# Store and load quarters alternate in a hex convolution kernel: 256 KB transfers, a semaphore for each stored quarter

## The chip, the cores and the metric

The kernel runs on one core of a Trainium2 chip. The metric is the device time of one execution in microseconds (us), as the median of several runs. The kernel before takes 740.97 us (three runs, 740.41 to 741.33).

## What is computed

The input x holds 2048 images of 64 channels and 16 x 16 pixels in float32 (134.2 MB). The output has the same shape.

```python
def _gn(v, G=32, eps=1e-5):                  # groups of two channels, over all pixels
    g = v.reshape(B_, G, C_ // G, H_, W_)
    m = jnp.mean(g, axis=(2, 3, 4), keepdims=True)
    s = jnp.var(g, axis=(2, 3, 4), keepdims=True)
    return ((g - m) / jnp.sqrt(s + eps)).reshape(v.shape)
...
xp = jnp.pad(x, ((0, 0), (0, 0), (1, 1), (1, 1)))
xp = xp.at[:, :, DST_R, DST_C].set(xp[:, :, SRC_R, SRC_C])      # 30 border pixels wrap round
up, left, right = (_conv(xp, w * mask, b) for ...)              # 4 x 4 taps, stride 2, 5 taps of each kept
out = zeros; out[0::2, 0::2] = up; out[1::2, 0::2] = left; out[1::2, 1::2] = right
return x + out * OUT_MASK
```

So every image is read once, normalised, convolved with three sparse stride-2 filters, and the results are added to the pixels of x that they belong to. All of x is written out, the unchanged pixels too.

## The kernel before, in words

**Chunks and slots.** The batch is cut into 64 chunks (NCHUNK) of 32 images. A chunk lies in SBUF as 128 partitions (2 images x 64 channels) by 16 "pairs" (G = 16) of 256 pixels: 1 KB of each partition for each pair, 2 MB for a chunk. The tensor xs has 8 such slots (SLOTS); chunk k lives in slot k % 8. The convolution's results are added in place in xs (L401), and the slot is then stored from there. So slot k % 8 can take chunk k + 8 only when chunk k has been stored.

**The engines.** For each chunk DVE takes the statistics (bn_stats, L229, a chunk ahead of the rest), works out scale and shift (L237 to L272) and normalises eight of the 16 pairs into tn (L277). ACT normalises the other eight (L313). POOL copies the wrapped border pixels (L411). PE runs the matmuls (L459). ACT carries the PSUM banks to res (L336), two chunks behind (LAG = 2), and POOL adds res into xs (L401). After the four banks of a chunk the semaphore bank_added stands at 4 * (k + 1).

**The transfers.** All transfers of x and of the output are issued by SP, in one order written out by hand (L182 to L214). First come three weight loads (L196), then chunk 0 in four quarters of 512 KB (L199), each with a semaphore that DVE waits on, then the chunks 1 to 6 in halves of 1 MB (AHEAD = 7). After that SP runs a loop over the chunks. For chunk k it stores half 0, loads half 0 of chunk n = k + 7, stores half 1, and loads half 1 of chunk n. The store waits for bank_added (L207). The load waits until both halves of the chunk that was in the slot, which is chunk k - 1, have been stored (L211): there is one semaphore for a slot, and it has to reach 32 for each turn. DVE waits for the half of a chunk whose statistics it takes (L224, L226). At the end SP waits for every slot's semaphore (L214).

The last chunk's two stores are not held to the same value: half 0 goes when the additions to its pairs are done and half 1 when those to the rest are.

Of the kernel before, what the change touches and what calls it, by code (L numbers as in the profile page):

```python
# [16 lines left out]
G = 16  # L17
NCHUNK = B // (2 * G)
SLOTS = 8
# [38 lines left out]
NB = len(BANKS)  # L58
# [3 lines left out]


QUARTER = G // 4
HALF = (slice(0, G // 2), slice(G // 2, G))
AHEAD = 7


# [16 lines left out]
def view(tensor, at, dims, first=0, parts=P):  # L85

    full = tensor[:, ]
    row = full.ap[0][0]
    return bass.AP(full.tensor, full.offset + first * row + at, [[row, parts]] + [list(d) for d in dims])


def hex_conv(nc, x, w_up, b_up, w_left, b_left, w_right, b_right, out):
    ctx = ExitStack()
    with ctx:
        def sb(name, shape, dt):
            return ctx.enter_context(nc.sbuf_tensor(name, shape, dt))

        def sem(name):
            return ctx.enter_context(nc.semaphore(name))

        x_dram = x.rearrange("(n g h) c r q -> n (h c) g (r q)", g=G, h=2)
        out_dram = out.rearrange("(n g h) c r q -> n (h c) g (r q)", g=G, h=2)

        xs = sb("xs", [P, SLOTS, G * PIX], F32)
# [21 lines left out]
        def w_raw(t):  # L126
            at = C * 16 * W_AT[t][1]
            return tn[1][W_AT[t][0]:W_AT[t][0] + C, at:at + C * 16]
# [3 lines left out]
            return tn[1][W_AT[t][0]:W_AT[t][0] + C, at:at + C]  # L132

        loaded = [[sem(f"loaded{s}_{half}") for s in range(SLOTS)] for half in range(2)]
        stored = [sem(f"stored{s}") for s in range(SLOTS)]
        w_loaded = [sem(f"w_loaded{t}") for t in range(3)]
        b_loaded = sem("b_loaded")
        quarter = [sem(f"quarter{n}") for n in range(2)]
        cleared = sem("cleared")
        identity = sem("identity")  # L140
        edges_clear = sem("edges_clear")
# [12 lines left out]
        bank_added = sem("bank_added")  # L154
# [26 lines left out]

        @block.sync  # L182
        def _(sp):
            def part(dram, k, pairs):
                return dram[k][:, pairs], xs[:, k % SLOTS, :].rearrange("p (g q) -> p g q", g=G)[:, pairs]

            def load(k, half):
                frm, to = part(x_dram, k, HALF[half])
                sp.dma_start(to, frm).then_inc(loaded[half][k % SLOTS], 16)

            def store(k, half):
                to, frm = part(out_dram, k, HALF[half])
                sp.dma_start(to, frm).then_inc(stored[k % SLOTS], 16)  # L193

            for t, w in enumerate((w_up, w_left, w_right)):
                sp.dma_start(w_raw(t), w.rearrange("o c a b -> o (c a b)")).then_inc(w_loaded[t], 16)  # L196
            for n in range(4):
                frm, to = part(x_dram, 0, slice(QUARTER * n, QUARTER * (n + 1)))
                sp.dma_start(to, frm).then_inc((quarter[n // 2], loaded[n // 2][0])[n % 2], 16)  # L199
            for k in range(1, AHEAD):  # L200
                for half in range(2):
                    load(k, half)

            for k in range(NCHUNK):
                n = k + AHEAD
                for half in range(2):
                    sp.wait_ge(bank_added, NB * (k + 1) if k < NCHUNK - 1 else NB * k + 4 + 2 * half)  # L207
                    store(k, half)
                    if n < NCHUNK:
                        if n >= SLOTS:  # L210
                            sp.wait_ge(stored[n % SLOTS], 32 * (n // SLOTS))  # L211
                        load(n, half)
            for s in range(SLOTS):
                sp.wait_ge(stored[s], 32 * (NCHUNK // SLOTS))  # L214

        @block.vector
        def _(dve):
            def bn(k, u0, u1):

                if k >= NCHUNK:  # L220
                    return
                s = k % SLOTS
                if k and u0 in (0, G // 4):
                    dve.wait_ge(loaded[4 * u0 // G][s], 16 * (k // SLOTS + 1))  # L224
                if k and u0 == 0 and u1 == G // 2:
                    dve.wait_ge(loaded[1][s], 16 * (k // SLOTS + 1))  # L226
                for u in range(u0, u1):
                    both = view(xs, (s * G + 2 * u) * PIX, [(1, PIX), (PIX, 2)])
                    last = nc.vector.bn_stats(stats[:, k % 2, 2 * u:2 * u + 2].rearrange("p g a -> p (g a)"), both)  # L229
                if u1 == G // 2:  # L230
                    last.then_inc(bn_done, 1)

            def moments(k, ahead):

                done = STAT_OPS * k
                own = stats[:, k % 2]
                nc.vector.stream_shuffle(mate[:].rearrange("p g a -> p (g a)"), own.rearrange("p g a -> p (g a)"),  # L237
                                         [p ^ 1 for p in range(32)]).then_inc(stat_step, 1)
                bn(ahead, 0, 1)
                dve.wait_ge(stat_step, done + 1)  # L240
                nc.vector.tensor_tensor(gap[:], own[:, :, 1], mate[:, :, 1], ALU.subtract).then_inc(stat_step, 1)
                nc.vector.tensor_tensor(m2[:], own[:, :, 2], mate[:, :, 2], ALU.add).then_inc(stat_step, 1)  # L242
                nc.vector.tensor_tensor(msum[:], own[:, :, 1], mate[:, :, 1], ALU.add).then_inc(stat_step, 1)  # L243
                dve.wait_ge(stat_step, done + 2)
                nc.vector.scalar_tensor_tensor(gap2[:], gap[:], float(PIX // 2), gap[:],  # L245
                                               op0=ALU.mult, op1=ALU.mult).then_inc(stat_step, 1)
                bn(ahead, 1, 2)
                dve.wait_ge(stat_step, done + 5)

                nc.vector.scalar_tensor_tensor(var[:], gap2[:], EPS * GROUP, m2[:],  # L250
                                               op0=ALU.add, op1=ALU.add).then_inc(var_ready, 1)
                bn(ahead, 2, 4)

            def norms(k, ahead):

                done = STAT_OPS * k + 5
                dve.wait_ge(std_ready, k + 1)
                nc.vector.reciprocal(small[:, 0], std[:]).then_inc(stat_step, 1)  # L258
                bn(ahead, 4, 5)
                dve.wait_ge(stat_step, done + 1)  # L260
                nc.vector.scalar_tensor_tensor(small[:, 1], var[:], -0.5 / GROUP, small[:, 0],  # L261
                                               op0=ALU.mult, op1=ALU.mult).then_inc(stat_step, 1)
                bn(ahead, 5, 6)
                dve.wait_ge(stat_step, done + 2)
                nc.vector.tensor_tensor(small[:, 2], small[:, 1], small[:, 0], ALU.mult).then_inc(stat_step, 1)  # L265
                bn(ahead, 6, 7)
                dve.wait_ge(stat_step, done + 3)
                nc.vector.scalar_tensor_tensor(rstd[:], small[:, 2], 1.5, small[:, 0],  # L268
                                               op0=ALU.add, op1=ALU.mult).then_inc(stat_step, 1)
                bn(ahead, 7, 8)  # L270
                dve.wait_ge(stat_step, done + 4)
                nc.vector.scalar_tensor_tensor(nmr[:], msum[:], -0.5, rstd[:],  # L272
                                               op0=ALU.mult, op1=ALU.mult).then_inc(norm_ready, 1)

            def t_pairs(b, s, g0, g1):
                for g in range(g0, g1):
                    last = nc.vector.tensor_scalar(t_image(b, g), x_image(s, g), rstd[:, g:g + 1], nmr[:, g:g + 1],  # L277
                                                   ALU.mult, ALU.add)
                return last

            def normalise(k, pairs=GD):
                dve.wait_ge(norm_ready, k + 1)
                wait_t_free(dve, k)
                t_pairs(k % 2, k % SLOTS, 0, pairs).then_inc(t_dve, 1)

            for n in range(4):
                dve.wait_ge((quarter[n // 2], loaded[n // 2][0])[n % 2], 16)
                bn(0, QUARTER // 2 * n, QUARTER // 2 * (n + 1))
            dve.wait_ge(bn_done, 1)
            moments(0, NCHUNK)  # L290
            norms(0, NCHUNK)
            normalise(0, GD0)
            bn(1, 0, G // 2)
            dve.wait_ge(bn_done, 2)

            for k in range(1, NCHUNK):
                moments(k, k + 1)
                norms(k, k + 1)
                normalise(k)
                if k + 1 < NCHUNK:  # L300
                    dve.wait_ge(bn_done, k + 2)
# [210 lines left out]
```

## Time and profile before

| what | value |
|---|---|
| median of three runs | 740.97 us (740.41 to 741.33) |
| the profiled execution's own time | 742.11 us |
| its span, from first to last instruction | 740.3 us |
| outside the span | 1.8 us |
| PE busy | 655.8 us (89%) |
| weight loads of PE | 602.8 us (81%) |
| DVE busy | 613.8 us (83%) |
| ACT busy | 574.8 us (78%) |
| POOL busy | 473.9 us (64%) |
| read from HBM, written to it | 135.01 MB, 134.22 MB |
| mean rate over the span | 364 GB/s |

The table gives the busy time of each engine in one profiled execution. The page of the profile also cuts the span into 40 slices and gives the transfer rate of each. The trace behind it can be asked for the rate in any stretch, for the issues on a queue in order of time, and for how long a transfer took from issue to landing. "Landing" is the last of the semaphore increments that the 16 DMA engines give when each has done its share. The page's "chain that ended last" is followed back from the last instruction; its entries for DMA say that work was waiting for a transfer.

### The profile page before, as it was taken

To read this page: it belongs to the slowest core of one execution; us is meant where nothing else is said; L and a number is where in the kernel's file an instruction comes from. 1 tells how busy PE (TensorE), PEld (TensorE's weight loads), DVE (VectorE), ACT (ScalarE), POOL (GpSimd) and SP (SyncE) were. 2 spreads that over 40 slices of the span, in tenths; PEclk is the share of its full clock that TensorE was granted. 3 is DMA by queue.
4 is the path that set the end of the run, shared out by engine and by line. 5 is a ranking of instruction groups with operands and counts; after the bars stand their busy time and mean duration, and the time that the engine had idled before them with its cause. 6 is when DMAs were issued, how large, how long until landed. Compare 5 with 4: busy or idle time off the path is not lost.

```text
span 740.3 us, 36046 instructions
## 1 busy us (share of the span) xinstructions
PE 655.8 (89%) x15484; PEld 602.8 (81%) x15484; DVE 613.8 (83%) x1793; ACT 574.8 (78%) x1235; POOL 473.9 (64%) x1109
## 2 busy tenths in 40 slices
PE   1699999999999989889889898898898988989893
PEld 1589999999999888778788787787887878878883
DVE  4999999999999778788787787887977878878740
ACT  3488888988888787787877877878778778787782
POOL 1177777787776765756657657566576575665774
PEclk9989999999999999999999999999999999999997
DMA  8999999999999999999999999999999999999998
GB/s 262 349 362 384 384 380 373 367 367 374 374 356 366 366 367 370 365 379 368 366 369 367 374 370 367 374 365 362 379 361 375 362 366 376 365 365 374 378 352 286
DMA packets 267034, 269.62 MB, mean 364 GB/s; under 512 B 4656, under 2 KB 266800, under 8 KB 266992
## 3 DMA queue, kind: packets, MB, share of 16 engines
q1 hardware_dynamic: 266512, 269.24, 106.0%
q14 instruction: 38, 0.31, 0.1%
q10 hardware_dynamic: 480, 0.00, 0.0%
q8 instruction: 4, 0.07, 0.0%
HBM read 135.01 MB, written 134.22 MB: 364 GB/s over the span
## 4 chain that ended last, share of the span: by engine, by line
DMA 36%; DVE 31%; ACT 12%; POOL 10%; SPq 4%; issue 3%; PE 3%; POOLq 0%; ACTq 0%
DMA xs<-in_x 35%; DVE stats L229 17%; ACT tn L313 12%; DVE tn L277 7%; POOL xs L401 5%; POOL tn L411 4%; SPq L193 3%; PE bank L459 3%; DVE small L261 2%; DMA out<-xs 1%; DVE nmr L272 1%; DVE small L265 1%; DVE rstd L268 1%; DVE var L250 1%; DVE mate L237 0%
## 5 line engine op out<-in xcount | busy, mean ns | idle before, releaser
L459 PE MATMUL bank<-tn,wts 64*64 64x192 f32 (+1 forms) x15360 | 646.9, 325 | 0.0
L459 PEld LDWEIGHTS bank<-tn,wts 64*64 64x64 f32 x15360 | 593.4, 137 | 34.1
L229 DVE BATCH_NORM_STATS2 stats<-xs 128x6 f32<-128x512 f32 x512 | 350.4, 697 | 95.1 <-DMA xs<-in_x 95.1
L401 POOL TENSOR_TENSOR xs<-res,xs 128x192 f32<-128x192 f32 (+6 forms) x775 | 376.1, 530 | 7.7 <-ACT res L336 5.8
L313 ACT ACTIVATE tn<-xs,nmr,rstd 128x256 f32<-128x256 f32 x511 | 258.9, 592 | 78.7 <-DVE nmr L272 78.1
L336 ACT ACTIVATE res<-bank,bias 64x512 f32<-64x512 f32 (+5 forms) x640 | 302.1, 472 | 21.1 <-PE bank L459 10.9
L411 POOL COPY tn<-tn 128x128 f32<-128x128 f32 (+2 forms) x320 | 97.3, 362 | 242.2 <-ACT tn L313 242.2
L277 DVE TENSOR_SCALAR tn<-xs,rstd,nmr 128x256 f32<-128x256 f32 x513 | 181.5, 427 | 2.3
L470 PEld LDWEIGHTS bank<-blank 128*128 128x128 f16 x64 | 6.1, 96 | 82.5 <-ACT res L336 65.8
L470 PE MATMUL bank<-blank 128*128 128x2 f16 x64 | 11.2, 176 | 63.9 <-POOL tn L411 63.8
L307 ACT ACTIVATE std<-var 128x16 f32<-128x16 f32 x64 | 13.8, 216 | 49.7 <-DVE var L250 49.7
L261 DVE SCALAR_TENSOR_TENSOR small<-var,small 128x16 f32<-128x16 f32 x64 | 26.4, 412 | 0.1
L265 DVE TENSOR_TENSOR small<-small 128x16 f32<-128x16 f32 x64 | 19.6, 306 | 0.1
L250 DVE SCALAR_TENSOR_TENSOR var<-gap,m 128x16 f32<-128x16 f32 x64 | 19.5, 304 | 0.1
L268 DVE SCALAR_TENSOR_TENSOR rstd<-small 128x16 f32<-128x16 f32 x64 | 18.1, 283 | 0.1
L258 DVE RECIPROCAL small<-std 128x16 f32<-128x16 f32 x64 | 14.8, 232 | 1.0 <-ACT std L307 1.0
L272 DVE SCALAR_TENSOR_TENSOR nmr<-msum,rstd 128x16 f32<-128x16 f32 x64 | 13.7, 214 | 0.1
L237 DVE STREAM_SHUFFLE mate<-stats 128x48 f32<-128x48 f32 x64 | 13.0, 204 | 0.0
L439 PE MATMUL bank<-ident,tn 64*64 64x64 f32 x60 | 3.5, 316 | 8.6 <-ACT tn L177 8.6
L242 DVE TENSOR_TENSOR m<-stats,mate 128x16 f32<-128x16 f32 x64 | 11.1, 173 | 0.0
L243 DVE TENSOR_TENSOR msum<-stats,mate 128x16 f32<-128x16 f32 x64 | 11.0, 172 | 0.0
L245 DVE SCALAR_TENSOR_TENSOR gap<-gap 128x16 f32<-128x16 f32 x64 | 10.7, 167 | 0.0
(18 smaller groups left out, 24.1 us busy)
## 6 DMA issues: line engine op xcount, KB each, us to landing
out<-xs SPq DMA_DIRECT2D x128, 1024.0 KB, 11.1
xs<-in_x SPq DMA_DIRECT2D x126, 1024.0 KB, 11.1
xs<-in_x SPq DMA_DIRECT2D x4, 512.0 KB, 8.4
tn<-in_L_conv_w_up SPq DMA_DIRECT2D x1, 256.0 KB, 3.8
tn<-in_L_conv_w_left SPq DMA_DIRECT2D x1, 256.0 KB, 4.3
tn<-in_L_conv_w_right SPq DMA_DIRECT2D x1, 256.0 KB, 6.2
bias<-in_L_conv_b_up ACTq DMA_DIRECT2D x2, 0.2 KB, 4.5
bias<-in_L_conv_b_left ACTq DMA_DIRECT2D x2, 0.2 KB, 6.0
```

The costliest lines, as they stand in the source:

```text
L193: sp.dma_start(to, frm).then_inc(stored[k % SLOTS], 16)
L229: last = nc.vector.bn_stats(stats[:, k % 2, 2 * u:2 * u + 2].rearrange("p g a -> p (g a)"), both)
L250: nc.vector.scalar_tensor_tensor(var[:], gap2[:], EPS * GROUP, m2[:], op0=ALU.add, op1=ALU.add).then_inc(var_ready, 1)
L261: nc.vector.scalar_tensor_tensor(small[:, 1], var[:], -0.5 / GROUP, small[:, 0], op0=ALU.mult, op1=ALU.mult).then_inc(stat_step, 1)
L265: nc.vector.tensor_tensor(small[:, 2], small[:, 1], small[:, 0], ALU.mult).then_inc(stat_step, 1)
L268: nc.vector.scalar_tensor_tensor(rstd[:], small[:, 2], 1.5, small[:, 0], op0=ALU.add, op1=ALU.mult).then_inc(stat_step, 1)
L277: last = nc.vector.tensor_scalar(t_image(b, g), x_image(s, g), rstd[:, g:g + 1], nmr[:, g:g + 1], ALU.mult, ALU.add)
L313: last = nc.scalar.activation(t_image(k % 2, g), x_image(k % SLOTS, g), ACT.Identity, bias=nmr[:, g:g + 1], scale=rstd[:, g:g + 1])
L336: last = nc.scalar.activation(res[onto, BANK_AT[j] + at:BANK_AT[j] + at + cols], psum[NB * b + j][banks, at:at + cols], ACT.Identity, bias ...
L401: last = nc.gpsimd.tensor_tensor(onto, frm, onto, ALU.add)
L411: last = nc.gpsimd.tensor_copy(view(tn[b], dst, [(T_PAIR, G)] + [(d, n) for d, _, n in dims]), view(tn[b], src, [(T_PAIR, G)] + [(d, n) fo ...
L459: last = nc.tensor.matmul(psum[bank + j][to:to + C, at:at + cols], wts[first:first + C, NT * rect[0] + n, :], taps(b, rect, tap, first), s ...
```

## The change

Three things change in SP's program, and the waits that go with them.

- The loop goes by quarters of a chunk (four pairs, 512 KB) instead of halves: store quarter q of chunk k, load quarter q of chunk k + 7, for q from 0 to 3.
- Every quarter is issued as two transfers of two pairs, 256 KB each (PIECES = 2). That makes 16 issues for a chunk instead of four. Chunk 0, too, is loaded in eight pieces of 256 KB instead of four of 512 KB.
- Each quarter of a slot has its own store semaphore. The load of quarter q of chunk k + 7 waits only for quarter q of chunk k - 1.

The semaphores of the loads stay by half, and count to 64 for each turn of a slot where they counted to 16. Nothing changes in what PE, ACT and POOL do, and DVE's waits stand where they stood. Helpers of the changed code are in the diff, which is cut to its core.

```diff
 QUARTER = G // 4
-HALF = (slice(0, G // 2), slice(G // 2, G))
+NQ = 4
+PIECES = 2
 AHEAD = 7
...
-        stored = [sem(f"stored{s}") for s in range(SLOTS)]
+        stored = [[sem(f"stored{s}_{q}") for s in range(SLOTS)] for q in range(NQ)]
...
-        quarter = [sem(f"quarter{n}") for n in range(2)]
+        quarter = [sem(f"quarter{q}") for q in range(NQ)]
...
-            def load(k, half):
-                frm, to = part(x_dram, k, HALF[half])
-                sp.dma_start(to, frm).then_inc(loaded[half][k % SLOTS], 16)
-
-            def store(k, half):
-                to, frm = part(out_dram, k, HALF[half])
-                sp.dma_start(to, frm).then_inc(stored[k % SLOTS], 16)
+            def pieces(dram, k, q):
+                n = QUARTER // PIECES
+                for at in range(QUARTER * q, QUARTER * (q + 1), n):
+                    pairs = slice(at, at + n)
+                    yield dram[k][:, pairs], xs[:, k % SLOTS, :].rearrange("p (g q) -> p g q", g=G)[:, pairs]
+
+            def load(k, q):
+                for frm, to in pieces(x_dram, k, q):
+                    sp.dma_start(to, frm).then_inc(loaded[q // 2][k % SLOTS], 16)
+
+            def store(k, q):
+                for to, frm in pieces(out_dram, k, q):
+                    sp.dma_start(to, frm).then_inc(stored[q][k % SLOTS], 16)
+
+            def wait_added(k, q):
+                sp.wait_ge(bank_added, NB * (k + 1) if k < NCHUNK - 1 else NB * k + 4 + 2 * (q // 2))
+
+            def wait_stored(k, q):
+
+                if k >= SLOTS:
+                    sp.wait_ge(stored[q][k % SLOTS], 16 * PIECES * (k // SLOTS))
...
             for k in range(NCHUNK):
                 n = k + AHEAD
-                for half in range(2):
-                    sp.wait_ge(bank_added, NB * (k + 1) if k < NCHUNK - 1 else NB * k + 4 + 2 * half)
-                    store(k, half)
+                for q in range(NQ):
+                    wait_added(k, q)
+                    store(k, q)
                     if n < NCHUNK:
-                        if n >= SLOTS:
-                            sp.wait_ge(stored[n % SLOTS], 32 * (n // SLOTS))
-                        load(n, half)
+                        wait_stored(n, q)
+                        load(n, q)
             for s in range(SLOTS):
-                sp.wait_ge(stored[s], 32 * (NCHUNK // SLOTS))
+                for q in range(NQ):
+                    sp.wait_ge(stored[q][s], 16 * PIECES * (NCHUNK // SLOTS))
...
+            def wait_loaded(k, half):
+
+                turns = k // SLOTS + (k % SLOTS > 0)
+                dve.wait_ge(loaded[half][k % SLOTS], 16 * 2 * PIECES * turns)
```

## Rows read from the trace of the kernel before

**Rows 1.** The page: rate of transfers in 40 slices, and its totals.
```profile
GB/s 262 349 362 384 384 380 373 367 367 374 374 356 366 366 367 370 365 379 368 366 369 367 374 370 367 374 365 362 379 361 375 362 366 376 365 365 374 378 352 286
q1 hardware_dynamic: 266512, 269.24, 106.0%
q10 hardware_dynamic: 480, 0.00, 0.0%
```

**Rows 2.** Stretches: length, busy us by engine, clock, DMA share, GB/s.
```profile
15.00:25.00 10.00, 1.94 (x21) 1.67 (x25) 9.43 (x30) 3.77 (x8) 1.50 (x5) 1.00 1.10 348
75.00:100.00 25.00, 25.00 (x636) 23.29 (x628) 24.93 (x73) 21.46 (x46) 17.47 (x41) 1.00 1.09 383
300.00:400.00 100.00, 89.73 (x2147) 82.77 (x2138) 83.14 (x251) 77.94 (x168) 62.81 (x150) 1.00 1.07 370
720.00:730.00 10.00, 8.29 (x216) 7.78 (x208) 0.00 (x0) 4.63 (x11) 6.62 (x15) 1.00 1.03 343
```

**Rows 3.** The chain in time: DVE's normalisation, chunk by chunk (start, us, what).
```profile
92.94 3.03 DVE tn L277 x8
...
102.92 3.10 DVE tn L277 x8
```

**Rows 4.** SP's own waits: what it waited for, us in total, times, longest.
```profile
SPq L189 <- DMA out<-xs: 168.6, 56, 3.3
SPq L214 <- DMA out<-xs: 5.1, 1, 5.1
```

**Rows 5.** SP's issues in order of time (start, us): early, steady, and the last load.
```profile
58.74 0.37 SPq L189 DMA_DIRECT2D xs<-in_x  x1
...
115.10 0.37 SPq L189 DMA_DIRECT2D xs<-in_x  x1
...
298.07 2.43 SPq L193 DMA_DIRECT2D out<-xs  x1
300.55 2.76 SPq L189 DMA_DIRECT2D xs<-in_x  x1
303.35 2.63 SPq L193 DMA_DIRECT2D out<-xs  x1
309.02 0.37 SPq L189 DMA_DIRECT2D xs<-in_x  x1
309.43 2.28 SPq L193 DMA_DIRECT2D out<-xs  x1
...
684.80 0.37 SPq L189 DMA_DIRECT2D xs<-in_x  x1
...
687.70 2.74 SPq L189 DMA_DIRECT2D xs<-in_x  x1
```

**Rows 6.** Issue to landing: the store of 298.07, then the load of 300.55.
```profile
DMA to landing us min/median/max: 10.9/10.9/10.9
...
DMA to landing us min/median/max: 11.2/11.2/11.2
```

**Rows 7.** Stretches inside one steady cycle, columns as in rows 2.
```profile
305.00:309.00 4.00, 3.43 (x113) 3.10 (x104) 4.00 (x16) 3.40 (x8) 1.17 (x4) 1.00 1.09 379
310.50:311.50 1.00, 1.00 (x24) 0.83 (x20) 0.00 (x0) 0.97 (x2) 1.00 (x3) 1.00 1.02 282
311.50:315.00 3.50, 3.50 (x78) 3.31 (x74) 3.28 (x8) 1.73 (x6) 3.50 (x9) 1.00 1.02 341
```

**Rows 8.** The head: chunk 0's quarters and the first 1 MB load (ns, starts; landing us).
```profile
L199 SPq DMA_DIRECT2D xs<-in_x x4: 508/555/1747, 2.6 to 4.4; - x4
...
DMA to landing us min/median/max: 6.9/8.4/9.7
...
L189 SPq DMA_DIRECT2D xs<-in_x x1: 2129/2129/2129, 6.2 to 6.2; - x1
```

**Rows 9.** The page: issues by kind, KB each, median us to landing.
```profile
xs<-in_x SPq DMA_DIRECT2D x126, 1024.0 KB, 11.1
xs<-in_x SPq DMA_DIRECT2D x4, 512.0 KB, 8.4
```

**Rows 10.** The end: DMA between the last stores, and the last store's landing.
```profile
731.00:732.00 1.00, 0.00 (x0) 0.00 (x0) 0.00 (x0) 0.15 (x1) 0.77 (x4) 1.00 0.28 98
...
DMA to landing us min/median/max: 5.7/5.7/5.7
```

More of the change, by code:

```diff
@@ L183, in _ @@
         def _(sp):
-            def part(dram, k, pairs):
-                return dram[k][:, pairs], xs[:, k % SLOTS, :].rearrange("p (g q) -> p g q", g=G)[:, pairs]
-            def load(k, half):
-                frm, to = part(x_dram, k, HALF[half])
-                sp.dma_start(to, frm).then_inc(loaded[half][k % SLOTS], 16)
-            def store(k, half):
-                to, frm = part(out_dram, k, HALF[half])
-                sp.dma_start(to, frm).then_inc(stored[k % SLOTS], 16)
+            def pieces(dram, k, q):
[3 more added lines that the diff above has]
+                    yield dram[k][:, pairs], xs[:, k % SLOTS, :].rearrange("p (g q) -> p g q", g=G)[:, pairs]
@@ L195, in _ @@
             for t, w in enumerate((w_up, w_left, w_right)):
                 sp.dma_start(w_raw(t), w.rearrange("o c a b -> o (c a b)")).then_inc(w_loaded[t], 16)
-            for n in range(4):
-                frm, to = part(x_dram, 0, slice(QUARTER * n, QUARTER * (n + 1)))
-                sp.dma_start(to, frm).then_inc((quarter[n // 2], loaded[n // 2][0])[n % 2], 16)
+            for q in range(NQ):
+                for frm, to in pieces(x_dram, 0, q):
+                    sp.dma_start(to, frm).then_inc(quarter[q], 16)
@@ L200, in _ @@
             for k in range(1, AHEAD):
-                for half in range(2):
-                    load(k, half)
+                for q in range(NQ):
+                    load(k, q)
             for k in range(NCHUNK):
                 n = k + AHEAD
-                for half in range(2):
-                    sp.wait_ge(bank_added, NB * (k + 1) if k < NCHUNK - 1 else NB * k + 4 + 2 * half)
-                    store(k, half)
+                for q in range(NQ):
+                    wait_added(k, q)
+                    store(k, q)
@@ L209, in _ @@
                     if n < NCHUNK:
-                        if n >= SLOTS:
-                            sp.wait_ge(stored[n % SLOTS], 32 * (n // SLOTS))
-                        load(n, half)
+                        wait_stored(n, q)
+                        load(n, q)
             for s in range(SLOTS):
-                sp.wait_ge(stored[s], 32 * (NCHUNK // SLOTS))
+                for q in range(NQ):
+                    sp.wait_ge(stored[q][s], 16 * PIECES * (NCHUNK // SLOTS))
         @block.vector
@@ L223, in bn @@
                 if k and u0 in (0, G // 4):
-                    dve.wait_ge(loaded[4 * u0 // G][s], 16 * (k // SLOTS + 1))
+                    wait_loaded(k, 4 * u0 // G)
                 if k and u0 == 0 and u1 == G // 2:
-                    dve.wait_ge(loaded[1][s], 16 * (k // SLOTS + 1))
+                    wait_loaded(k, 1)
                 for u in range(u0, u1):
@@ L284, in normalise @@
                 t_pairs(k % 2, k % SLOTS, 0, pairs).then_inc(t_dve, 1)
-            for n in range(4):
-                dve.wait_ge((quarter[n // 2], loaded[n // 2][0])[n % 2], 16)
-                bn(0, QUARTER // 2 * n, QUARTER // 2 * (n + 1))
+            for q in range(NQ):
+                dve.wait_ge(quarter[q], 16 * PIECES)
+                bn(0, QUARTER // 2 * q, QUARTER // 2 * (q + 1))
             dve.wait_ge(bn_done, 1)
```

## Prediction

> **What bounds the kernel now.** I read the transfer rate first. After the first slices the page shows 350 to 380 GB/s in every slice but the last [rows 1], so the DMA engines look busy from end to end. The next question is whether the arithmetic could go faster. It could: DVE's normalisation starts at 92.94 and again at 102.92 us [rows 3], one chunk in 10.0 us while the first loads still gave it a lead, and PE is busy for the whole of that stretch [rows 2]. In the steady part SP's issues repeat every 11.4 us (309.02 us is one of them), and PE falls to 90% [rows 2, 5]. A chunk moves 4 x 1.049 = 4.19 MB, and 4.19 MB in 11.4 us is 368 GB/s. So transfers set the pace of some 57 chunks, those that both load and store, and arithmetic sets none of it until the last load has landed, at 687.70 + 11.1 = 698.8 us [rows 5, 9]. From there on 41 us of arithmetic and the last stores remain. The DMA engines even run nearly dry in that tail, at 98 GB/s in one microsecond [rows 10].
>
> Then I looked inside one steady cycle. SP issues store, load, store back to back from 298.07 to 305.98 us, stands for 3.0 us, and issues the next load at 309.02 [rows 5]. That is L211: half 0 of a load waits for both halves of the chunk before. The store issued at 298.07 took 10.9 us to land, at 308.97, which is what released it [rows 5, 6]. Over the run this wait comes to 168.6 us in 56 times [rows 4]. While SP stands, the rate holds at 379 GB/s, because 2 MB are queued behind the awaited store. It falls only 1.5 us after the release: 282 GB/s for 1 us, then 341 for 3.5 us [rows 7]. Between 75 and 100 us the same wait makes no such hole, and the rate is 383 GB/s [rows 2]. A hole under a queue that still holds 2 MB for the last of the 16 DMA engines can only mean that some engines had run ahead of it and were empty.
>
> The early stretch agrees. There the engines move 383 GB/s, but SP's cycle, which is held by the landing of the last engine, is (115.10 - 58.74)/5 = 11.27 us, or 372 GB/s [rows 2, 5]. The difference is a lead that the other engines gain over one late engine. A transfer counts as landed only when the late one is done.
>
> **The change, part by part.**
>
> *The store semaphores by quarter.* The load of quarter q now waits for a store that stands a whole chunk back in the queue: eight quarter transfers (4 MB) lie between the two, where today there are two halves (2 MB). SP's issues also block when the queue is full. In the steady part the store issued at 309.43 ends at 311.71, just when the load of 300.55 lands (300.55 + 11.2 [rows 5, 6]). Three transfers, or 3 MB, are then outstanding. So the queue should fill to 3 MB before the new wait is reached, the wait of 3.0 us disappears, and what SP waits for instead is room in the queue. The ahead-running engines keep 3 MB less their lead in place of 2 MB less their lead, and the hole goes or comes later. Behind the waiting load stand SP's later stores and loads alone, and no engine waits for SP except through a landing.
>
> What is that worth? If the late engine had been starved, the whole hole would come back. But it has 2 MB in its queue when SP is released, so it is never empty. Its own pace is the limit, and the nearest row of that pace without a hole is the early 11.27 us. From 115.10 to 684.80 us there are 50 chunks in 569.7 us, 11.39 us each [rows 5]. At 11.27 they would take 563.6: **6.1 us saved**. The bounds are 0 (the late engine doesn't notice) and 26 us (57 chunks at the early rate, 4.19 MB / 383 GB/s = 10.95 us, instead of 11.4). I take the 6.1, since its row measures the landing of the last engine and the other measures the mean of all.
>
> *16 transfers in place of four, on the DMA engines.* The bytes and the 1 KB packets stay (266512 packets for 269.24 MB is 1.0 KB each [rows 1]). Each transfer ends with one more small packet on each engine. 480 packets of the bias loads took 0.0% of 16 engines' time [rows 1], so under 0.05% of 16 x 740.3 us = 5.9 us, or under 12.3 ns each. Twelve more for each of 57 chunks are 684 on each engine, so the cost is between 0 and 8.4 us. No row separates the two ends, and I take the middle, **4.2 us**. What a transfer costs beyond the packet has a weak bound from the head. The quarters of 512 KB issued at 2.6 and 4.4 us landed after 6.9 and 9.7 us, so three of them in 4.6 us, 1.5 us each, which is the 348 GB/s of the 1 MB loads that follow [rows 2, 8]. No cost shows. But loads alone are slower than the mix, so a stall of one engine could hide there.
>
> The Trainium skill speaks against this part: "DMA: Bandwidth & Descriptors", section "Rules for kernel authors", wants at least 1 MiB in a transfer for full bandwidth. Its section on the anatomy of a transfer puts the fixed 2 us mostly in waiting for the completion. The trace shows that transfers overlap (four are in flight at 11.1 us each), so I expect this cost to stay hidden. The sum above doesn't use the rule.
>
> *The same on SP.* An issue that isn't blocked takes 0.37 us for 1 MB and 0.51 to 0.56 for most of the 512 KB ones [rows 5, 8]. Sixteen of them are 6 to 9 us in a cycle of 11.3 us. They hide behind the queue, with 2 us to spare at the worst. The cover is gone at 0.71 us an issue.
>
> *The depth of the queue.* It must be 3 MB and not three or four transfers. At the end of the first 1 MB issue (6.15 + 2.13 = 8.28 us) all four quarters were still out, the first landing only at 2.6 + 6.9 = 9.5 us [rows 8]. That is five transfers and 3 MB, against three transfers and 3 MB later. So bytes fit and a count doesn't. Twelve in the queue at once is not shown.
>
> *Head and tail.* Eight issues for chunk 0 take about 4.4 us, while their landing goes on to 14 us: nothing. DVE's waits count higher and stay where they were; half 0 of a load still ends halfway through its chunk. The last store's 1 MB (5.7 us to landing [rows 10]) goes as four pieces at the same rate: nothing, or at most 0.5 us either way. The 24 more waits at the end stand inside the 5.1 us that SP waits there anyway [rows 4].
>
> The sum is 742.1 - 6.1 + 4.2 = 740.2 us against the profiled execution's own time. That lies 1.1 us above the median of the runs, so **739.1 us**. With the packets at either of their bounds this case reaches from 735 to 743.
>
> **The rivals.**
>
> *1. The holes were the loss, and the late engine goes with the others.* Then mixed chunks run at the early 383 GB/s: 742.1 - 26 - 1.1 = 715 us. For it: the early slices ran so for 50 us [rows 1], and a shorter burst of stores may suit the late engine better. Against it: the landings of that same stretch came every 11.27 us and not 10.95.
>
> *2. Slower: each added completion costs the late engine its full time, and its pace isn't helped.* This takes place at the end of each 256 KB piece on the engine that sets the landing. 742.1 + 8.4 - 1.1 = 749 us. It decides from about 9 ns a piece, 6.1 us over 684, when the relief is there, and at once when it is not. If a piece cost 20 ns, the time would be 755 without relief. For it: the late engine is never empty, so all that is added to it lengthens the cycle. Against it: the quarters of the head show nothing.
>
> *3. The queue holds few transfers after all, or SP's issue is the bound.* With 1 MB in flight, less than the 2 MB at which holes open today, the holes would be deeper and the time over 770 us. At 0.8 us an issue SP alone would need 12.8 us a chunk: 742.1 + 57 x 1.4 = 822 us. The five in flight and the 0.5 us issues speak against both.
>
> *4. It doesn't do what it says.* The 3.0 us wait goes and is replaced one for one by blocked issues, and no byte moves sooner: 741 us.
>
> **How the numbers follow.** Differences under 0.2% (1.5 us) can't be told from none here. Forecast 0.45, of which faster 0.25, within 0.15, slower 0.05. Rival 1 has 0.20 (faster), rival 2 0.27 (slower), rival 3 0.05 (slower), rival 4 0.03 (within). That makes faster 0.45, same 0.18, slower 0.37. Both signs hold much of it. The forecast's own range is 735 to 743. The whole range reaches from rival 1 to beyond rival 2: 715 to 752. Left out are rival 3, the dearer part of rival 2 and a little under 715, some 0.15.
>
> **What would show it.** SP's wait on stores in the profile after should fall from 168.6 us to nearly nothing, and issues should be blocked instead. The rate in 300 to 400 us should be flatter. If the landings then come every 11.3 us, the late engine is the limit. At 10.95 it is rival 1. At over 11.4 with a full queue it is the price of the pieces. Landings of pieces much under 8 us after issue would mean a shallow queue. I would be most wrong if small pieces changed the packet rate itself, which no row of before measures in the mix.

## The result

The changed kernel takes 746.72 us (median of four runs, 745.60 to 747.88) against 740.88 us for the kernel before on the same chip: 1.0079 times as long, 95% interval 1.0062 to 1.0096. It is 5.8 us slower. The forecast was 739.1 us, on the other side, though the time lies within its range of 715 to 752. The profiled execution of the changed kernel took 747.88 us, its span 746.1 us.

From the page of the changed kernel: the rate in 40 slices, the queue's total, and the issues by kind (KB each, median us to landing).

```profile
GB/s 266 348 361 382 382 383 364 371 351 361 378 363 361 363 372 368 366 373 356 373 374 369 369 355 369 372 363 365 360 374 369 368 366 355 376 371 362 377 346 260
...
q1 hardware_dynamic: 278768, 269.29, 106.1%
...
xs<-in_x SPq DMA_DIRECT2D x512, 256.0 KB, 5.3
out<-xs SPq DMA_DIRECT2D x512, 256.0 KB, 5.5
```

The bytes are those of [rows 1]. The 12256 packets more are completions: 766 more transfers of x and the output (1024 in place of 258) on 16 engines. Landing takes half of the 11.1 us of [rows 9].

SP's own waits in the changed kernel (us in total, times, longest):

```profile
SPq L197 <- POOL xs L418: 21.1, 39, 4.6
SPq L226 <- DMA out<-xs: 1.6, 2, 1.5
```

And some of SP's issues in order of time (start, us; x2 is one quarter in two pieces):

```profile
299.42 1.22 SPq L197 DMA_DIRECT2D out<-xs  x2
300.68 1.27 SPq L193 DMA_DIRECT2D xs<-in_x  x2
301.99 1.15 SPq L197 DMA_DIRECT2D out<-xs  x2
303.19 1.68 SPq L193 DMA_DIRECT2D xs<-in_x  x2
```

The wait of 168.6 us for stores [rows 4] is gone, and SP stands in blocked issues instead: a store's takes 0.60 us in the median (0.37 at the least, 1.29 at the most), a load's 0.65 (0.47 at the least). The change does what it says. But the rate didn't rise with it. Here are the stretches of [rows 2] again, and between them one that is worse (370 GB/s before).

```profile
75.00:100.00 25.00, 25.00 (x623) 22.97 (x619) 24.93 (x71) 21.55 (x45) 18.45 (x42) 1.00 1.09 382
150.00:200.00 50.00, 50.00 (x1207) 46.08 (x1199) 49.82 (x139) 43.59 (x95) 36.89 (x84) 1.00 1.07 361
300.00:400.00 100.00, 89.61 (x2121) 82.94 (x2123) 81.12 (x245) 78.08 (x167) 63.63 (x150) 1.00 1.07 368
```

In what follows, the *pace* is the time a chunk takes between the first store of chunk 8 and that of chunk 56, from SP's issues. Before, these start at 132.22 and 678.97 us, 11.391 us a chunk. In the changed kernel:

```profile
135.39 0.47 SPq L197 DMA_DIRECT2D out<-xs  x1
...
685.57 0.65 SPq L197 DMA_DIRECT2D out<-xs  x1
```

That is 550.18/48 = 11.462 us: 0.071 us more, 3.4 us over the 48 chunks. At chunk 8 SP is 3.2 us later than before, but little of that is time lost: 2.0 us stand there at the first store already (45.17 us, where it was 43.15), which SP reaches later because its queue is shallower, and up to 130 us both kernels move the same, 356 GB/s before and 355 after.

The whole 5.8 us can be followed on the chain that ended last. The last load lands at 703.4 us in place of 698.9, 4.6 us later. Behind it stand the last arithmetic and the last stores, and there PE's last convolution but one took 1.3 us longer than the 9.98 us before:

```profile
712.75 11.27 PE bank L476 x179
```

In 3.4 of these 11.27 us (713.1 to 716.5) the granted clock was 0.50, the lower of the two levels; before it was 1.00 up to the end of the last convolution. So of the 5.8 us between the two profiled executions 4.6 are the transfers' and some 1.3 the clock's. Whether the other three executions had that dip isn't shown; the profiled one is the longest of the four.

### The profile page after: what moved, and what is told of

It reads as the page before. It is cut to its first block, busy times and chain, and to the rows that moved or that the text cites. A ratio compares the mean times of both kernels' runs of the same rounds, so it can differ in the third digit from the quotient of the medians.

```text
span 746.1 us, 36824 instructions
## 1 busy us (share of the span) xinstructions
PE 658.0 (88%) x15484; PEld 605.8 (81%) x15484; DVE 611.8 (82%) x1793; ACT 574.4 (77%) x1235; POOL 471.7 (63%) x1109
## 4 chain that ended last, share of the span: by engine, by line
SPq 43%; DVE 28%; DMA 8%; POOL 7%; issue 5%; ACT 5%; PE 3%; POOLq 0%; ACTq 0%
SPq L193 23%; SPq L197 19%; DVE stats L246 14%; DMA xs<-in_x 8%; DVE tn L294 7%; POOL xs L418 6%; ACT tn L330 4%; PE bank L476 3%; POOL tn L428 2%; DVE small L278 1%; DVE small L282 1%; DVE rstd L285 1%; DVE nmr L289 1%; SPq L211 1%; DVE mate L254 1%
## 5 line engine op out<-in xcount | busy, mean ns | idle before, releaser
L294 DVE TENSOR_SCALAR tn<-xs,rstd,nmr 128x256 f32<-128x256 f32 x513 | 179.0, 422 | 2.3
L282 DVE TENSOR_TENSOR small<-small 128x16 f32<-128x16 f32 x64 | 22.0, 343 | 0.1
L289 DVE SCALAR_TENSOR_TENSOR nmr<-msum,rstd 128x16 f32<-128x16 f32 x64 | 12.2, 190 | 0.1
L259 DVE TENSOR_TENSOR m<-stats,mate 128x16 f32<-128x16 f32 x64 | 11.1, 173 | 0.0
L258 DVE TENSOR_TENSOR gap<-stats,mate 128x16 f32<-128x16 f32 x64 | 10.4, 162 | 0.1
```

## The experiments

Theory A of the expectations is the prediction's relief; theory B says that the awaited store cost nothing. All medians are compared with the kernel before, run beside them (741.2 to 741.5 us; 740.88 beside the change itself, so a difference to its 746.72 us can be off by half a microsecond). The diffs are against the kernel named and cut to their core.

**Each half its own store semaphore**, 1 MB transfers, against the kernel before:

```diff
-                sp.dma_start(to, frm).then_inc(stored[k % SLOTS], 16)
+                sp.dma_start(to, frm).then_inc(stored[half][k % SLOTS], 16)
...
-                            sp.wait_ge(stored[n % SLOTS], 32 * (n // SLOTS))
+                            sp.wait_ge(stored[half][n % SLOTS], 16 * (n // SLOTS))
```

> The kernel before with one thing undone: each half of a slot has its own store semaphore, the transfers stay at 1 MB (four a chunk). The wait of 3.0 us for the store before should go, with the queue 3 MB deep. Theory A (the relief is real, and the change ate it because its 256 KB pieces fill the queue at some eight transfers, 2 MB, so that the engines that run ahead are empty as before): this kernel is faster, 735 us (740.9 less the 6.1 us of the prediction), with a chunk every 11.27 us. Theory B (the late DMA engine is never empty, so the wait costs nothing and its removal gives nothing; the 5.8 us lost are the price of 684 more transfers on that engine): 740.9 us within 1 us, SP's wait on stores gone, and still a chunk every 11.39 us.

Measured: 741.35 us, ratio 0.9998 (0.9989 to 1.0007). Its profile no longer has the wait for stores. Landing takes 11.3 us (the page's median) and the pace is (678.36 - 131.99)/48 = 11.383 us. The stretch from 300 to 400 us:

```profile
300.00:400.00 100.00, 89.33 (x2141) 82.59 (x2132) 83.76 (x251) 77.86 (x168) 62.79 (x151) 1.00 1.07 369
```

The reader should see 369 GB/s where [rows 2] had 370. SP's issues follow each other within 0.06 us from 45 to 680 us, but for two gaps of 0.4 us, and yet the rate still dips as in [rows 7], here with SP in the middle of its issues:

```profile
304.00:305.00 1.00, 1.00 (x38) 1.00 (x31) 1.00 (x4) 1.00 (x3) 0.00 (x0) 1.00 0.91 309
```

A wait of 168.6 us went, the queue was kept full, and nothing followed. Theory A has fallen, and the dips aren't made by that wait.

**Quarters as single transfers of 512 KB**, against the changed kernel (`PIECES = 1`):

> The changed kernel with each quarter as one transfer of 512 KB (eight a chunk, a semaphore for each stored quarter). Theory A: six transfers fit the 3 MB queue, so the relief is there: 735 to 738 us. Theory B: the price goes by the number of transfers, four more a chunk in place of twelve, a third of the 5.8 us: 742.8 us.

Measured: 735.65 us, ratio 0.9922 (0.9908 to 0.9935), 5.8 us faster than before. Neither theory holds: B expected 742.8, and A's number comes out although its cause is gone, which is luck. The pace is (674.31 - 133.43)/48 = 11.268 us, and the rate is up in the same stretch.

```profile
300.00:400.00 100.00, 89.90 (x2147) 83.19 (x2143) 83.52 (x251) 78.82 (x168) 63.71 (x151) 1.00 1.08 375
```

Early on it is faster still. The first stores of chunks 1 and 5 start at 55.38 and 98.93 us, 10.89 us a chunk, beside the same arithmetic. So the 11.27 us that the kernel before has there isn't a pace that some engine has of itself.

**The pieces alone**: order, halves and the slot's one semaphore as before, each half in four transfers of 256 KB (`cut` gives four slices of two pairs; stores likewise).

```diff
-                frm, to = part(x_dram, k, HALF[half])
-                sp.dma_start(to, frm).then_inc(loaded[half][k % SLOTS], 16)
+                for pairs in cut(half):
+                    frm, to = part(x_dram, k, pairs)
+                    sp.dma_start(to, frm).then_inc(loaded[half][k % SLOTS], 16)
```

> The pieces alone: order, halves and the slot's one store semaphore as in the kernel before, but each half is issued as four transfers of 256 KB (16 a chunk). Theory A: the old wait comes on top of a queue of only 2 MB, so the holes are deeper than in the changed kernel: 750 us or more. Theory B: the wait costs nothing and the number of transfers is that of the changed kernel, so the time is too: 746.7 us within 1 us. A third theory, that the finer alternation of loads and stores is what costs, expects 741 us here, since loads and stores alternate by 1 MB as before.

Measured: 751.31 us, ratio 1.0134 (1.0119 to 1.0150). So the pieces cost 9.9 us by themselves, and the rest of the change gives some of it back. The third theory, that finer alternation is what costs, is refuted with its sign turned, and theory B's 746.7 us is missed by 4.6. (SP's wait for stores is 23.1 us here, 0.6 at the longest, so it isn't the deeper holes of theory A either.)

**Alternation and number, told apart.** From here on theory C: alternating loads and stores more finely gains, and each transfer costs. Three kernels hold one and move the other. The first is the changed kernel with store and load in turn by single 256 KB pieces, with a store semaphore for each eighth. The second is that of 512 KB transfers with this order:

```diff
-                for q in range(NQ):
-                    wait_added(k, q)
-                    store(k, q)
-                    if n < NCHUNK:
-                        wait_stored(n, q)
-                        load(n, q)
+                for half in (0, 2):
+                    for q in (half, half + 1):
+                        wait_added(k, q)
+                        store(k, q)
+                    if n < NCHUNK:
+                        for q in (half, half + 1):
+                            wait_stored(n, q)
+                            load(n, q)
```

The third is the kernel of the half semaphores, which stores both halves and then loads both.

> The changed kernel, the same 16 transfers of 256 KB a chunk, but loads and stores alternate by single transfers instead of by two (each eighth of a slot has its own store semaphore). So far alternation by 1 MB gave 741 us with four transfers a chunk and 751 us with 16, and alternation by 512 KB gave 735.7 us with eight and 746.7 us with 16. Theory C (finer alternation gains, the number of transfers costs): another gain here, 740 us or less. Theory D (the gain of the 512 KB kernel is no matter of alternation but of the size of a transfer, with 256 KB too small for the queue): 746.7 us within 1 us.

> Transfers of 512 KB, eight a chunk, with a semaphore for each stored quarter, but two stores follow each other and then two loads, so that loads and stores alternate by 1 MB as in the kernel before. Theory C: the gain goes and four more transfers a chunk cost 14.5 ns each (9.9 us over 684, from the halves in four pieces), 741.4 + 3.3 = 744.7 us. Theory D: 735.7 us, as when they alternate by 512 KB.

> Transfers of 1 MB, four a chunk, a semaphore for each stored half, but both halves are stored and then both are loaded, so that they alternate by 2 MB. Theory C: coarser alternation loses about what finer gained (5.8 us and more), 747 to 755 us. Theory D: 741.4 us.

Measured: 740.37 us (0.9991, 0.9982 to 1.0000), 744.76 us (1.0049, 1.0036 to 1.0062) and 757.35 us (1.0222, 1.0196 to 1.0248). The first two came within 0.4 us of what theory C expected, and the last 2.4 us beyond the range it gave. Side by side, in us:

| transfers a chunk | alternate by 2 MB | by 1 MB | by 512 KB | by 256 KB |
|---|---|---|---|---|
| 4 of 1 MB | 757.35 | 741.35 | | |
| 8 of 512 KB | | 744.76 | 735.65 | |
| 16 of 256 KB | | 751.31 (old wait) | 746.72 (the change) | 740.37 |

Along a row the alternation gets finer and every step gains: 16.0, 9.1, 4.6 and 6.4 us. Down a column the transfers get more and every step costs: 3.4, 6.6 and 11.1 us. SP isn't the cause: in none of these kernels does it stand more than 0.6 us between two issues from 45 to 680 us, neither for the additions nor for a store. The rates follow. From 300 to 400 us the kernel of 744.76 us:

```profile
300.00:400.00 100.00, 89.55 (x2136) 82.60 (x2130) 81.02 (x246) 77.94 (x168) 62.72 (x147) 1.00 1.07 365
```

And that of 757.35 us:

```profile
300.00:400.00 100.00, 86.83 (x2067) 79.50 (x2063) 85.34 (x243) 75.28 (x161) 63.27 (x144) 1.00 1.06 362
```

**Which completions cost.** The changed kernel with only its stores, or only its loads, in 256 KB pieces, the others whole at 512 KB:

> The changed kernel with each loaded quarter as one transfer of 512 KB and each stored one as two of 256 KB: 12 transfers a chunk, alternation by 512 KB as before. Between 735.7 us (both at 512 KB) and 746.7 us (both at 256 KB). If the completion of a store costs and that of a load hardly does: 745 us or more. If the number counts: 741.2. If loads are what costs: 737.

> The other way round: each stored quarter as one transfer of 512 KB, each loaded one as two of 256 KB, 12 transfers a chunk. If the completion of a store is what costs: 737 us. If the number counts: 741.2. If loads: 745 or more.

Measured: 742.54 us (1.0020, 1.0012 to 1.0029) and 739.74 us (0.9979, 0.9970 to 0.9990). Over the 735.65 us of whole quarters these are 6.9 and 4.1 us, together 11.0, which is the 11.1 of both at once. So the price adds up: 256 stores more at 27 ns, 256 loads more at 16 ns. It isn't the stores' alone. Whether it goes by the number of transfers or by their size this pair can't tell. In the column of alternation by 1 MB it goes by the number: 13 ns for each of 256 more at 512 KB, and 13 ns for each of 768 more at 256 KB.

**The transfers without arithmetic**, in halves as before, in the pieces of the change, and in 512 KB quarters:

> Leaves out all arithmetic and the weight loads: SP loads each chunk and stores it again unchanged, in the halves, the order and with the slot's one store semaphore of the kernel before (a store waits for its load in place of the additions). If the late engine's pace is the transfers' own, a chunk still takes 11.3 to 11.4 us and the run 64 x 11.4 = 730 us or somewhat less, since no arithmetic follows the last load. If the arithmetic's traffic in SBUF slows the transfers, a chunk takes about 10.9 us (385 GB/s) and the run under 710 us.

> The same without arithmetic in the form of the changed kernel: quarters alternate, two transfers of 256 KB each, a semaphore for each stored quarter. If each transfer costs the late engine its completion (5.8 us over 684 more transfers, 8.5 ns), this run is 5 to 6 us longer than the one in halves. If the loss of the changed kernel comes from the meeting of its finer transfers with the arithmetic, the two are the same within 1 us.

> Without arithmetic: 512 KB quarters that alternate, eight transfers a chunk. The halves took 708.6 us, 256 KB pieces 715.1. If alternation gains only where arithmetic disturbs the transfers, this run shows the price of four more transfers a chunk alone: 708.6 + 6.5/3 = 710.8 us. If finer alternation gains by itself, it is under 708 us.

Measured: 708.59, 715.07 and 710.03 us. In halves the pace is (646.91 - 124.84)/48 = 10.877 us, and the rate stays at 384 to 386 GB/s in all slices but the first three and the last two, although SP waits for stores here too (143.7 us in 56 times). The page's rate of the halves:

```profile
GB/s 301 348 364 384 384 385 386 386 386 386 386 386 385 386 386 386 386 386 386 386 386 386 386 386 386 386 386 386 386 386 386 386 386 386 386 386 386 386 365 309
```

My first guess, that the pace of 11.39 was the late engine's own, is refuted. Without arithmetic nothing is lost to holes, 768 transfers more cost 6.5 us (8.4 ns each), and the finer alternation of the quarters gives at most 0.8 us (710.03 against the 710.8 expected without a gain). The gain by alternation exists only where arithmetic disturbs the transfers, and there a transfer also costs one and a half to three times as much.

**Which arithmetic.** First the kernel before with one tap of each filter's five, then the transfers with PE's matmuls on zeros beside them and no other arithmetic:

> The kernel before with one tap of each filter's five (the convolution's other four are left out): PE's matmuls and its reads of SBUF fall to a fifth, all else stays. If PE's traffic is what slows the late DMA engine from 10.88 us a chunk without arithmetic to 11.39, a chunk takes 10.9 to 11.0 us here and the run 710 to 715 us (with a shorter tail too, some 15 us, so down to 698). If it is DVE, ACT or POOL, the pace stays 11.39 and only the tail is shorter: 725 us or so.

> The transfers of the kernel before (halves, one queue, one store semaphore a slot) with PE's matmuls on zeros beside them and no other arithmetic; nothing waits for PE. Without any arithmetic a chunk took 10.88 us and the run 708.6. If PE's reads of SBUF are what slows the late engine, a chunk takes 11.2 to 11.4 us and the run 725 to 738. If PE matters only through the rest of the arithmetic that follows its pace, 10.9 us and 709 to 711.

Measured: 721.21 us and 727.16 us. The first lies between the two times expected, while its pace is nearly that of PE's branch. The paces are (659.97 - 131.08)/48 = 11.019 us and (665.30 - 126.65)/48 = 11.222 us. PE alone takes the pace from 10.88 to 11.22, two thirds of the way to 11.39, and without four fifths of its matmuls it falls from 11.39 to 11.02. The same stretch with one tap:

```profile
300.00:400.00 100.00, 30.17 (x441) 24.87 (x441) 84.42 (x258) 80.57 (x173) 64.88 (x153) 0.57 1.08 382
```

And with PE alone (the columns are PE, its weight loads and POOL), in the same stretch and in two early ones:

```profile
300.00:400.00 100.00, 100.00 (x2403) 92.18 (x2398) 0.00 (x0) 1.00 1.08 375
80.00:100.00 20.00, 20.00 (x486) 18.41 (x482) 0.00 (x0) 1.00 1.09 385
140.00:160.00 20.00, 20.00 (x484) 18.41 (x480) 0.00 (x0) 1.00 1.07 372
```

So PE's matmuls make up most of the loss, and yet they aren't enough for it: PE is busy without a pause from 40 us on, and from 60 to 110 us the transfers keep the 385 GB/s that they have without any arithmetic. The loss sets in between 100 and 120 us, in the whole kernels too (the fall from 384 to 373 in [rows 1], the end of the 10.89 us a chunk with 512 KB quarters). What else is needed was not found. In the one-tap kernel PE waits a lot and its mean granted clock is 0.57 of full, without harm to the pace.

**128 KB pieces**, the changed kernel with `PIECES = 4`:

> The changed kernel with four transfers of 128 KB a quarter, 32 a chunk. By the price of 8.5 ns a transfer it would take 5.8 + 16 x 57 x 0.0085 = 13.6 us over the kernel before, 754 us. If the queue holds about eight transfers, only 1 MB is queued, and if an issue takes 0.37 us with 0.04 us between, SP alone needs 32 x 0.41 = 13.1 us a chunk: then 840 us and more, and SP is the bound.

Measured once: 1014.15 us. The row gives min, median and max ns of an issue.

```profile
L197 SPq DMA_DIRECT2D out<-xs x1024: 332/435/942, 61.1 to 1010.0; - x171
```

From chunk 8 to chunk 56 an issue takes 0.445 us in the mean, with 0.043 us between two: 32 of them are 15.6 us a chunk, and the pace is 15.7 us. SP never stands, the rate is 269 GB/s, and PE is 73% busy from 300 to 400 us. SP is the bound, as the third rival had it for dearer issues. So 256 KB is near the end of what one queue can issue.

**Two queues.** If alternation is what gains, it should be finest where the engines have a load and a store to take from at any time. The first kernel moves the stores, 1 MB each, to ACT's queue. The second also spaces them, and leaves those of the last seven chunks to SP:

```diff
                     evacuate(k - LAG, k % 2, j)
+                    if j == 1 and LAG + 1 < k <= LAST + LAG + 1:
+                        store(k - LAG - 2, 1)
+                if LAG < k <= LAST + LAG:
+                    store(k - LAG - 1, 0)
```

> Loads stay on SP's queue in halves of 1 MB, stores of 1 MB go through ACT's queue (issued when ACT has passed its wait for the additions of that chunk), so the DMA engines always have a load and a store to take from and may alternate by single packets; four transfers a chunk, a semaphore for each stored half. Theory C (finer alternation gains, each transfer costs): the gain of 512 KB over 1 MB and more with the fewest transfers, under 735 us, down to 710 us if the pace becomes that of the transfers without arithmetic (10.88 us a chunk). If the gain of finer alternation comes only from SP's one queue being shorter, nothing here: 741 us. ACT gets two issues of 0.4 us a chunk, which it can hide at 78% busy.

> As e10 (1 MB loads on SP's queue, 1 MB stores on ACT's, a semaphore for each stored half), but ACT issues the two stores of a chunk some 6 us apart, so that its queue has room for each, and SP issues those of the last seven chunks, as in the kernel before, when its loads are out. Theory C: the transfers keep the 385 GB/s of e10 and ACT is no longer blocked, so a chunk takes 10.9 us, 0.5 us less over 57 chunks: 741.4 - 28 = 713 us, up to 725 if ACT's issues cost it some of that. If e10 was slow for another reason than ACT's blocked issues, no better than 735 us.

Measured: 743.91 us (1.0030, 1.0020 to 1.0040) and 732.40 us (0.9881, 0.9867 to 0.9896), the fastest kernel here. In both the transfers ran at 385 to 386 GB/s from 75 to 345 us, beside all the arithmetic, and at 378 to 381 from 400 to 600 us. Whether finer alternation does that, or that two queues hold more transfers between them, was not told apart. But here are two issues on ACT's queue, one after the other, in the first kernel (start, us):

```profile
308.53 0.38 ACTq L313 DMA_DIRECT2D out<-xs  x1
...
308.94 3.27 ACTq L313 DMA_DIRECT2D out<-xs  x1
```

The second store's issue held ACT for 3.3 us (4.2 at the longest in the run). Over the run ACT's normalisation waited 113.9 us in 53 times for nothing but its own queue, and what the transfers had gained was lost there. My expectation that ACT gets two issues of 0.4 us, which it can hide, was wrong there. Spacing the stores brings that wait down, not away. The spaced kernel's waits (who, for what: us in total, times, longest):

```profile
ACT tn L312 <- issue: 76.3, 39, 2.9
```

And its stretch from 300 to 400 us:

```profile
300.00:400.00 100.00, 95.05 (x2226) 86.93 (x2217) 97.46 (x255) 79.93 (x174) 67.89 (x153) 0.97 1.08 383
```

It keeps 9 us of the 28 expected.

## Why the prediction was wrong, point by point

**What bounds the kernel.** Right in the main: transfers set the pace, and without arithmetic they run at 10.88 us a chunk. The early 383 GB/s was rightly read as what the engines can do. But the reading of the dips in [rows 7], that SP's wait leaves the engines that ran ahead empty, doesn't hold: without the wait, and with a queue that is full all the time, the dips and the 369 GB/s stay.

**The store semaphores by quarter.** This is the step that failed. "6.1 us saved" rested on the early pace of 11.27 us, taken as that of a late engine beside no holes. The half semaphores took the wait away and the pace stayed at 11.38. The prediction had named the reason itself: the late engine "is never empty", so the end of SP's wait could not help it. It should have drawn the conclusion and taken the lower bound, 0. What differs between the early stretch and the steady one isn't that wait. Nor was 11.27 us a pace of the late engine's own: with 512 KB quarters the same stretch takes 10.89 us a chunk. That those quarters later settle at 11.268 is a coincidence.

**The depth of the queue.** "Bytes fit and a count doesn't" was too strong. In steady blocked issue, the landing time over the time of one transfer (pace by number) gives 11.3/2.85 = 4.0 transfers of 1 MB, 8.1/1.41 = 5.8 of 512 KB and 5.4/0.716 = 7.5 of 256 KB, each with the one just being issued: 4.0, 2.9 and 1.9 MB. Smaller transfers make the queue shallower. But the depth didn't decide: with the same 16 transfers, the kernel that alternates by 256 KB is 6.4 us faster than the change.

**16 transfers in place of four.** The mechanism was right and the size off. 4.2 us were taken, with a bound of 8.4. The runs show 9.9 us for 12 more a chunk where they alternate by 1 MB, and 11.1 us for eight more where they alternate by 512 KB. The bound came from the bias loads' small packets: 8.4 ns a transfer is what it costs without arithmetic, but with it 13 to 27 ns. The warning of the Trainium skill ("DMA: Bandwidth & Descriptors", section "Rules for kernel authors", at least 1 MiB a transfer) points the right way for the number of transfers. By itself it would have rejected the 512 KB kernel, which is 0.8% faster than the one with 1 MB. There the measurement decides. The section of the Trainium skill on the anatomy of a transfer, which the prediction also cites, is about transfers issued from GpSimd; here SP issues them.

**What was left out.** The change alternates by 512 KB in place of 1 MB. The prediction gave that no term; the comparison at eight transfers shows 9.1 us for it. The sum by the runs, from the kernel before: 0 for the wait, +3.4 for the transfers four to eight at 1 MB, -9.1 for the alternation, +11.1 for eight to 16 make +5.4. Measured are +5.8.

**The rivals.** The second, slower by the completions without relief, came nearest: 749 us against 746.7. What it said of the wait held, and it deserved more than 0.27. That its number is so near is in part luck: it charged 8.4 us for the transfers, which cost 3.4 + 11.1, and left out the 9.1 us that the alternation gives back. The first was right that the rate of the early stretch can be won back in part (375 GB/s by alternation with 512 KB transfers, 383 by two queues), but not by this change. The issue on SP was costed rightly at nothing. So was the head, and of the tail the last stores: from the last chunk's first store to the end of the span it is 8.0 us in both. What the tail had beyond that was PE's clock, 1.3 us, which no term foresaw.

**What stays open.** Why arithmetic, PE's above all, slows the transfers, and why finer alternation softens that, was not shown. That one of the 16 engines is late was argued from the rate and the cycle, and the trace shows another picture. It holds the time of each of the 16 increments of a transfer. From 200 to 650 us in the kernel before, the first comes 3.5 us ahead of the last in the median, the eleventh still 2.6, and the next four 1.6, 1.1, 0.9 and 0.7. So some eleven engines are ahead together and five are behind them, spread over 1.6 us, not one alone. Without arithmetic the first is ahead by 1.6 us and the eleventh by 0.4. Which engines they are, no row names. With the half semaphores, where SP never stands, the first is 3.9 us ahead, and why the ones ahead then don't move more is open. So is what sets in after 100 us. Why a transfer costs 13 ns when they alternate by 1 MB and 22 ns by 512 KB is open as well.

## What to carry to other kernels

When loads and stores share a queue and their sum sets the pace, the size of a transfer and the grain of their alternation are two settings: move one at a time. Here the best on one queue was alternation by single transfers of 512 KB, and a change that got the alternation right lost it again by cutting each transfer in two. A long wait on the issuing engine is no loss as long as the engine that sets the pace has work queued through it, so ask that before crediting its removal.

## What was unexpected of the hardware

- The same transfers run at 386 GB/s alone and at 370 beside the arithmetic. PE's matmuls alone bring them to 375, although no transfer waits for PE, and not from its start: from 60 to 110 us they still run at 385 with PE fully busy.
- Loads on SP's queue and stores on ACT's, 1 MB each, kept 385 GB/s beside all the arithmetic for over 200 us, where one queue gave 362 to 375 from 300 to 400 us. A blocked issue on ACT's queue holds ACT itself, for up to 4.2 us (4.5 with the stores spaced).
- A transfer more cost 8.4 ns without arithmetic and 13 to 27 ns with it.
- With 128 KB transfers SP was the bound at 0.44 us an issue, and the kernel took 1014 us.
- The 16 increments of a 1 MB transfer lie 3.5 us apart from first to last beside the arithmetic, and 1.6 us without it.
